# A gated cross-attention and mixture-of-experts block: first feed-forward rounded through 16-bit integers, bias table on VectorE, shared results stored from two buffers

## What is computed

```
act_qdq(x): scale = max(max|x| / 32767, 1e-12); clip(round(x / scale), -32768, 32767) * scale
x = act_qdq(x)
up = act_qdq(x @ lpbq_dequant(w_up).T)
gate = act_qdq(x @ lpbq_dequant(w_gate).T)
sig = clip(round(sigmoid(gate) * 65536), 0, 65535) / 65536
gate = act_qdq(gate * sig)
o = act_qdq(gate * up)
return o @ lpbq_dequant(w_down).T
```

## Time and profile before

| | |
|---|---|
| median of 3 runs | 1800.84 us (1798.96 to 1802.85) |
| profiled execution, its own time | 1801.27 us |
| its span in the trace | 1799.5 us |
| TensorE matmul busy | 1422.7 us (79%) |
| VectorE busy | 1245.4 us (69%) |
| ScalarE busy | 1138.1 us (63%) |
| GpSimd busy | 244.2 us (14%) |
| 770 to 862 us, first feed-forward, rounding | TensorE 0.00, VectorE 71.80, ScalarE 62.34, GpSimd 14.12 us busy of 92 |
| 1460 to 1587 us, shared expert from step 10 | TensorE 75.01, VectorE 76.90, ScalarE 56.36 us busy of 127 |
| 1587 to 1799 us, routed experts | TensorE 196.27 us busy of 212 |

### The profile page before, as it was taken

How to read it: one execution, slowest core, us unless ns; L and a number is a source line. 1 busy time by engine, 2 the same in 40 slices (tenths; PEclk the granted TensorE clock), 3 DMA queues, 4 the chain that set the end, 5 groups by cost and what they waited for, 6 DMA issues and landing times. The chain is left out here.

```text
span 1799.5 us, 40814 instructions
## 1 busy us (share of the span) xinstructions
PE 1422.7 (79%) x15436; PEld 1013.3 (56%) x15436; DVE 1245.4 (69%) x3030; ACT 1138.1 (63%) x2422; POOL 244.2 (14%) x202
## 2 busy tenths in 40 slices
PE   1799999999999954900738889898898476779996
PEld 1566676766766643500725666666665354558885
DVE  6567777777677777478447889888887676534443
ACT  5466666666666633465436888888887444546664
POOL 4400001000010013020050000000000004024443
PEclk9999999999999986955857999999998687879998
DMA  4110000100010010000010001011000424522222
GB/s 145 35 36 19 19 19 19 36 19 19 19 27 18 2 54 1 0 0 0 10 42 22 24 25 31 17 31 32 17 26 4 127 64 130 175 42 44 46 46 28
DMA packets 36652, 66.09 MB, mean 37 GB/s; under 512 B 5161, under 2 KB 25618, under 8 KB 36466
## 3 DMA queue, kind: packets, MB, share of 16 engines
q1 hardware_dynamic: 27890, 53.40, 9.7%
q0 software_dynamic: 8576, 10.10, 3.6%
HBM read 48.16 MB, written 16.24 MB: 36 GB/s over the span
## 5 line engine op out<-in xcount | busy, mean ns | idle before, releaser
L519 ACT ACTIVATE a_pt<-a_ps_t 125x336 f16<-125x336 f32 x256 | 102.6, 448 | 107.5 <-PE a_ps_t L450 107.2
L1180 ACT ACTIVATE a_p<-a_s,a_nb 112x375 f32<-112x375 f32 x256 | 140.9, 598 | 26.9 <-DVE a_nb L1281 26.0
L291 PE MATMUL a_ps_o<-a_vh,a_pt 125*128 125x64 f16 (+1 forms) x1536 | 153.2, 183 | 3.0 <-ACT a_pt L1193 0.8
L293 PE MATMUL a_ps_o<-a_vh,a_pt 125*128 125x64 f16 (+1 forms) x1536 | 151.3, 182 | 0.0
L292 PE MATMUL a_ps_o<-a_vl,a_pt 125*128 125x64 f16 (+1 forms) x1536 | 151.2, 182 | 0.0
L1105 PE MATMUL a_ps_t<-ident,a_p 112*128 112x112 f32 x768 | 119.4, 287 | 39.8 <-ACT a_p L1180 39.3
L511 ACT ACTIVATE a_p<-a_ps_s,a_nb 112x375 f32<-112x375 f32 x256 | 144.1, 573 | 3.0 <-DVE a_scaled L591 3.0
L291 PEld LDWEIGHTS a_ps_o<-a_vh,a_pt 125*128 125x128 f16 x1536 | 133.8, 98 | 15.7 <-ACT a_pt L1193 7.5
L292 PEld LDWEIGHTS a_ps_o<-a_vl,a_pt 125*128 125x128 f16 x1536 | 131.2, 98 | 11.2
L1272 DVE TENSOR_TENSOR a_s<-a_ps_s,a_mask 112x750 f32<-112x750 f32 x128 | 119.8, 936 | 25.4 <-PE a_ps_s L1095 20.4
L1105 PEld LDWEIGHTS a_ps_t<-ident,a_p 112*128 112x128 f32 x768 | 81.2, 148 | 95.1 <-issue 80.2
(11 more groups left out here) (366 smaller groups left out, 4656.4 us busy)
## 6 DMA issues: line engine op xcount, KB each, us to landing
m_stage<-in_w SPq DMA_DIRECT2D x36, 512.0 KB, 4.2
a_ctx<-in_ctxT SPq DMA_DIRECT2D x16, 375.0 KB, 3.6
ctx<-a_cx SPq DMA_DIRECT2D x16, 375.0 KB, 4.3
a_cx<-ctx SPq DMA_DIRECT2D x16, 375.0 KB, 3.7
a_mask<-in_mask SPq DMA_DIRECT2D x16, 164.1 KB, 2.3
x_res<-in_x SPq DMA_DIRECT2D x1, 1792.0 KB, 9.5
out_x<-x_res SPq DMA_DIRECT2D x16, 112.0 KB, 2.2
normed_rows<-x_res SPq DMA_DIRECT2D x4, 448.0 KB, 5.1
```

What stands on the lines that cost most here:

```text
L291: nc.tensor.matmul(out, wh, mh, start=(i == 0), stop=False)
L293: last = nc.tensor.matmul(out, wl, mh, start=False, stop=(i == n - 1))
L519: nc.scalar.activation(pt[:, g % 2, i, 0, :, 0:S], ps_t[0:KV, i, 0:NKV * S].rearrange("p (t s) -> p t s", t=NKV), ACT.Copy).then_inc(pt_hi, 1)
L1180: nc.scalar.activation(p32[:, g % 2, i, 0:NC], s2[:, g % 2, i, :], ACT.Exp, bias=nb[:, g % 2, i:i + 1], scale=-1.0).then_inc(exp_done, 1)
```

## The change

**First feed-forward.** The jobs are reordered: all 24 of the gate first, then all 24 of up, written out in place of loops. Rounding is done by writing to 16-bit integers: a conversion takes the place of plus and minus MAGIC. New tiles are g_int and u_int (int16, [128, 6, 1792]) and sig_int (uint16, a ring of two). The gate's scale is made after the gate's 24 jobs, and ScalarE's rounding and sigmoid of the gate stand one by one behind the copies 28 to 39. VectorE's gated products stand between the largest magnitudes of up. U is rounded by ScalarE, GpSimd keeps only the four maxima over partitions. The last stage goes by 8 pieces of 224 columns: ScalarE rounds to int16, VectorE makes both parts (halves of U's storage).

```diff
@@ feed_forward0_phase, ScalarE
-            with act.Fori(0, NG) as g:
-                for j in range(NJ):
...
-                nc.scalar.activation(G[:, o, :], G[:, o, :], ACT.Identity, bias=m_c[:], scale=sc[:, 2:3]
-                                     ).then_inc(g_rounded, 1)
+            def round_gate(o):
+                if o == 0:
+                    act.wait_ge(scal, 1)
+                nc.scalar.activation(g_int[:, o, :], G[:, o, :], ACT.Copy, scale=sc[:, 2:3]).then_inc(g_rounded, 1)
+            def sigmoid(o):
+                act.wait_ge(g_rounded, o + 1)
+                wait(act, sig_rounded, o - 1)
+                nc.scalar.activation(sig[:, o % 2, :], g_int[:, o, :], ACT.Sigmoid, scale=sc[:, 3:4]
+                                     ).then_inc(sig_raw, 1)
+            for n in range(NJ + AHEAD):
+                take(n)
+            extra = [(f, o) for o in range(OC0) for f in (round_gate, sigmoid)]
+            for n in range(NJ + AHEAD, 2 * NJ):
+                take(n)
+                if extra:
+                    f, o = extra.pop(0)
+                    f(o)
...
+            act.wait_ge(scal, 2)
             for o in range(OC0):
+                nc.scalar.activation(u_int[:, o, :], U[:, o, :], ACT.Copy, scale=sc[:, 1:2]).then_inc(u_rounded, 1)
+            act.wait_ge(scal, 3)
+            for o in range(OC0):
+                nc.scalar.activation(g_int[:, o, :], G[:, o, :], ACT.Copy, scale=sc[:, 5:6]).then_inc(g2_rounded, 1)
+            act.wait_ge(scal, 4)
+            for g in range(NP2):
+                cc = slice(g * W2, (g + 1) * W2)
+                nc.scalar.activation(u_int[:, :, cc], G[:, :, cc], ACT.Copy, scale=sc[:, 7:8]).then_inc(o_rounded, 1)
@@ VectorE
+            def gated_product(o):
+                dve.wait_ge(sig_raw, o + 1)
+                nc.vector.tensor_scalar(sig_int[:, o % 2, :], sig[:, o % 2, :], UQ, UQ - 1.0, ALU.mult, ALU.min
+                                        ).then_inc(sig_rounded, 1)
+                dve.wait_ge(sig_rounded, o + 1)
+                nc.vector.tensor_tensor(G[:, o, :], sig_int[:, o % 2, :], g_int[:, o, :], ALU.mult).then_inc(gated, 1)
+                dve.wait_ge(gated, 2 * o + 1)
+                nc.vector.tensor_reduce(omx[:, 0, o:o + 1], G[:, o, :], AX.X, ALU.max, apply_absolute_value=True
+                                        ).then_inc(gated, 1)
...
+                nc.vector.tensor_tensor(G[:, o, :], u_int[:, o, :], g_int[:, o, :], ALU.mult).then_inc(multiplied, 1)
...
+            for g in range(NP2):
+                rounded = u_int[:, :, g * W2:(g + 1) * W2]
+                dve.wait_ge(o_rounded, g + 1)
+                nc.vector.tensor_copy(oh[:, g], rounded).then_inc(o_hi, 1)
                 dve.wait_ge(o_hi, g + 1)
+                nc.vector.tensor_tensor(ol[:, g], rounded, oh[:, g], ALU.subtract).then_inc(o_split, 1)
                 if g >= 1:
+                    add_down(g - 1)
```

```diff
@@ moe_front_phase, SyncE
-            sp.wait_ge(stored, 16 * NG)
@@ GpSimd
             pool.wait_ge(rows_out, 16 * NG)
+            def add_shared(g):
+                pool.wait_ge(added, TG * (g + 1))
+                nc.gpsimd.dma_start(out[g * TG:(g + 1) * TG].rearrange("t p d -> p t d"), y[g % 2], accum_op=ALU.add
+                                    ).then_inc(stored[g % 2], 16)
+
+            add_shared(0)
             pool.wait_ge(index_ready, 1)
...
-            for g in range(NG):
+            for g in range(1, NG):
                 add_shared(g)
@@ VectorE, add(g)
-                wait(dve, stored, 16 * g)
+                wait(dve, stored[g % 2], 16 * (g // 2))
@@ VectorE, step n
+                if n == 10:
+                    place_tile(1, part16[:, 0])
+                    place_tile(2, part16[:, 1])
                 if n == 11:
+                    place_tile(0, token[:])
+                if n in (12, 13):
+                    place_row(n - 12)
...
+                j = n - FIND_AT - 4
+                if 0 <= j < HC1:
+                    bias(nc.vector.tensor_tensor(bsel, tile_hot[:],
+                                                 b1[:, 0:E, j].unsqueeze(1).to_broadcast([128, MAXT, E]), ALU.mult))
+                    bias(nc.vector.tensor_reduce(tile_b1[:, :, j], bsel, AX.X, ALU.add))
@@ routed_experts_phase, GpSimd
+            for landed in stored:
+                pool.wait_ge(landed, 16 * (NG // 2))
```

More of the change, by code:

```diff
@@ L665, in feed_forward0_phase, with job @@
+        NJ = NG * OC0
         KU = 1.0 / WS
+        GATE, UP, GATED, OUT = range(4)
         block = ctx.enter_context(nc.Block())
+        def job(n):
+            m, r = divmod(n, NJ)
+            g, o = divmod(r, OC0)
+            return m, g, o
         @block.tensor
         def _(pe):
-            def group(g):
-                for j in range(NJ):
[L672 to L678, removed]
@@ L680, in _ @@
-            group(0)
-            with pe.Fori(1, NG) as g:
-                group(g)
+            for n in range(2 * NJ):
+                m, g, o = job(n)
+                w = (wgt, wup)[m]
+                wait(pe, copied, n - 5)
+                products(nc, pj[:, n % 6, 0:GW], [
+                    (w[:, 0, k, o * 128:(o + 1) * 128], w[:, 1, k, o * 128:(o + 1) * 128],
+                     xh[:, k, g * GW:(g + 1) * GW], xl[:, k, g * GW:(g + 1) * GW]) for k in range(KD)]
+                ).then_inc(job_done, 1)
@@ L683, in _ @@
             for t in range(B):
-                g = t // TG
+                g, i = divmod(t, 2)
                 pe.wait_ge(o_split, g + 1)
[L686 to L689, removed]
+                wait(pe, x_done, t - 1)
+                products(nc, po[0:S, t % 2, 0:D], [
                     (oh[:, g, o, i * S:(i + 1) * S], ol[:, g, o, i * S:(i + 1) * S],
-                     wdn[:, 0, o, :], wdn[:, 1, o, :]) for o in range(OC0)])
@@ L692, in _ @@
[L692 to L702, removed]
+                     wdn[:, 0, o, :], wdn[:, 1, o, :]) for o in range(OC0)]).then_inc(down_done, 1)
@@ L728, in _, with take @@
[L728 to L734 removed]
+            def take(n):
+                m, g, o = job(n)
+                act.wait_ge(job_done, n + 1)
+                nc.scalar.activation((G, U)[m][:, o, g * GW:(g + 1) * GW], pj[:, n % 6, 0:GW], ACT.Copy
+                                     ).then_inc(copied, 1)
@@ L792, in _ @@
+            for n in range(NG):
+                largest(n)
+            largest_of_all(GATE)
             link(nc.vector.tensor_scalar(sc[:, 0:1], sx[:], KU, None, ALU.mult))
-            scale_of(am[:, 0:1], sc[:, 0:1], sc[:, 4:5], sc[:, 1:2])
-            scale_of(am[:, 1:2], sc[:, 0:1], sc[:, 3:4], sc[:, 2:3])
+            dve.wait_ge(mx_all, 1)
+            link(scale_of(am[:, GATE:GATE + 1], sc[:, 0:1], sc[:, 3:4], sc[:, 2:3]))
             nc.vector.tensor_scalar(sc[:, 9:10], sc[:, 3:4], 1.0 / UQ, None, ALU.mult).then_inc(scal, 1)
-            for o in range(OC0):
-                dve.wait_ge(g_rounded, o + 1)
-                nc.vector.tensor_scalar(G[:, o, :], G[:, o, :], -MAGIC, None, ALU.add).then_inc(g_int, 1)
-                if o >= 1:
-                    gated(dve, link, o - 1)
@@ L814, in _ @@
[L814 to L821 removed]
+                product(o)
```

208 lines of the change are left out of this document (82 added, 126 removed).

## The result

The changed kernel takes **1751.82 us** (median of 4 runs, 1750.48 to 1756.27); the kernel before took 1801.13 beside it (4 runs). The ratio is 0.9731, 95% interval 0.971 to 0.9752. Forecast were 1752 us and a range of 1740 to 1765. The profiled execution took 1750.57 us, with a span of 1748.8 us.

The account below looks back on a forecast made before the run. It saw TensorE idling before the first feed-forward's down products behind ScalarE and VectorE chains, and in shared-expert stalls. Gains 33.3 + 12 + 3.4 = 48.7 off 1801.27 gave 1752.6, less 0.4 for the median: 1752 us, range 1740 to 1765.

Parts of the forecast that it names:

- 1 to 3: First feed-forward: early gate scale lets rounding start at 744.4 instead of 772.57; second scale at 794.0; copies end at 776.
- 4: First feed-forward: ScalarE rounds U from 787.0 to 797.4, past the second scale, so this is late next; first product 799.1.
- 5: First feed-forward: six products take 24.04 us as before, bounded by VectorE; third scale at 825.0, 28.8 us earlier.
- rival of cheap products: VectorE, first feed-forward: 16-bit sources make twelve products cost 1.0 instead of 2.0, 9 us reaching the end: 1743; chance 0.08.
- 6: First feed-forward's last stage: first low part after 3.7 us instead of 8.2; gain with the earlier scale 33.3 us.
- 7: Shared expert: spreading VectorE's patterns gains 0 (bounds -2 to +4.6), as the find then waits 3.6 us for row patterns.
- 8: Shared expert: bias table off GpSimd and results sent at once, so the second result waits for nothing; gain 12 us.
- 9: Shared expert: bias table on VectorE, 0.9 us a step in eight steps, costs 0 (bounds 0 and 7.2).
- 10: Shared expert's end: release at VectorE's last split, 1579.54, instead of the landing, 1582.88; gain 3.4 us, GpSimd's new wait costs 0.
- ScalarE slow with int16: First feed-forward: ScalarE writes or reads int16 slowly; gain eaten from 2.5 times the price, 1824 at 3; chance 0.03.
- 16-bit slow on VectorE: First feed-forward: 16-bit operands run at one-source half rate, 3.8 reaching the end and casts +0.7: 1757; chance 0.12.
- the weight stream binds: Shared expert: at weight landings of 6 us steps take 2.83, 0.4 more in each of 20, 8 us: 1760; chance 0.12.

Follow-up runs that it names:

- e9: The changed kernel with ScalarE rounding four blocks of U, then alternating gated-product and U blocks once the gated product's scale is there; 1747.57 us.
- e1: The kernel before with the changed first feed-forward alone; 1765.79 us, ratio 0.9809.
- e5: The changed kernel with the 0/1 patterns back in one piece ahead of step 10 and the find back at step 12; 1753.66 us.
- e7: The changed kernel with the find two steps later, at step 16 instead of 14; 1748.00 us.
- e6: The changed kernel with the bias table back on GpSimd, two result buffers and the sends at once kept; 1758.42 us.
- e8: The changed kernel with the bias table left out, its sixteen VectorE instructions replaced by one memset to zero; 1750.19 us.
- e11: The changed kernel with VectorE moving a group's result ahead of the step's low part and split instead of behind them; 1739.87 us.
- e3: The changed kernel with SyncE's wait for all four landings put back at the phase's end; 1749.35 us.
- e12: The changed kernel with three edits together: roundings reordered, find at step 16, a group's result moved first; 1738.17 us.
- e4: The changed kernel with the fourth result sent by GpSimd as its first work of the next phase; 1748.47 us.

## Why the prediction was right

Step by step, forecast against the profile after. First feed-forward:

- *1 to 3.* First rounding 744.4, was 745.38; second scale 794.0, was 793.36; copies end 776, were done at 776.2. The three instructions of a gated product took 1.09, 2.03 and 2.02, the 32-bit prices. VectorE waited 3.09 and 0.65 us where 2.9 and 0.9 were reckoned. One table load of 1.28 with the sigmoid right behind it; the 1.38 us of draining that the Trainium skill (ScalarE: Activation LUTs, What ACT_TABLE_LOAD costs) counts besides is in no row here either.
- *4.* U's roundings forecast 787.0 to 797.4, were 786.60 to 796.78; the first product 799.1, was 798.49. e9 shows that they were what was late.
- *5.* Six products 24.04, were 24.05: 16-bit sources with a 32-bit destination are no cheaper. The rival of cheap products fell. By the Trainium skill (Vector Engine (DVE) Microarchitecture Reference, 5.1 Performance modes) sources and destination must all be 16-bit for the double rate; the trace agrees, with 2.03 us for 1792 elements as with 32-bit sources.
- *6.* From the third scale's use to the first low part 3.7, was 2.92 (824.27 to 827.19). Cast and low part took 0.51 and 0.86 where I had 0.8 and 1.5. The estimate from the Trainium skill (VectorE: DVE Perf Modes, The perf-mode tier table), 0.4 and 0.8, was nearer. Gain forecast 33.3, was 34.95; e1 gives 35.0.

Shared expert:

- *7.* Gain 0, and the find's wait in its place: right (e5, e7), though the wait was 2.6 us, not 3.6.
- *8.* 12 us, mid-phase. Counted from the first pattern, the second result was moved 56.1 us later before, and 43.8 to 45.8 later in the kernels with the change, so 10.4 to 12.3 us: right. e6 adds how it splits.
- *9.* Cost 0: right (e8). A pair took 1.1 us, not 0.9, since the multiply with b1's column took 0.65.
- *10.* **Gain 3.4: wrong, it was about 0.** The chain's row of the landing and SyncE's wait had two readings. I took the wait that the change removes for the holder, and 1582.88 for the landing; that is the release, and the send landed 5.4 us behind its issue, at about 1582.3. GpSimd's drain ended at the same moment and stayed. The trace of before had it, in the rows of the line that ends the phase, and the prediction did not use them. The release fell at 1532.23 and not behind the last split at 1529.20, and the sign named for this step, TensorE's transposes 3.6 us behind that split, was not there: it was 6.7. The other half of the step held: GpSimd's new wait costs nothing, the first scatter comes 22.5 us behind the first transpose, before 22.7.

So the mechanisms of nine steps held and the tenth did not, and the sum of 48.7 met 49.3 partly by luck: 3.4 too much in step 10, 1.7 too little in the feed-forward (0.8 of it in step 6), 1.2 to 1.7 not counted in the norm behind it, and the rest scatter. Of the rivals, none came true. *ScalarE slow with int16* and *16-bit slow on VectorE* fell to the rows above; *the weight stream binds* did not hold in the changed kernel (ScalarE's longest wait for a landing in the shared expert was 1.9 us), but as soon as e11 took out the next stall, ScalarE waited up to 4.2 us for a landing at the phase's end; *the waiting only moved* fell to the first scatter's row.

## What to carry over

When two things end at the same moment, removing one of them buys nothing: before a wait at a phase's end is counted as gain, look at every queue's last row there, the drains too. A value range that fits 16 bits lets a rounding engine write integers directly, which saves the constant's extra passes at no price on ScalarE (1.78 us a block either way); on VectorE only the instructions with all operands in 16 bits became faster. And work moved to an engine's slack is free only as long as the engine's order lets what others wait for go first: moving one call (e11) was worth 11 us.

## What was not expected of the hardware

- GpSimd's drain at a phase's end lasts until its own last DMA has landed: 5.69, 5.51 and 5.61 us (after, before, e3) behind sends that took 5.4 to 5.6 to land, 9.6 us in e11 behind a send that took 9.5.
- A VectorE instruction beside GpSimd can lose far more than its own length: 0.18 became 2.53 us (e6).
- 16-bit VectorE work, 1344 elements: 0.51 us for an int16 to fp16 cast, 0.38 ns an element, against 0.60 ns (1.07 us for 1792) for one 32-bit source; 0.86 us for the difference of two 16-bit sources, 0.64 ns, against 1.13.
- TensorE starts 3.6 us behind this phase's release (before and after), 3.7 in e11 and e12, and 4.9 in e4. Why e4's start is later is open.
